# Ratio attention with double-buffered tiles, and its reciprocal as a logarithm, an exponential and a Newton step

## What is computed

```python
qkv = layernorm(x) @ w_qkv + b_qkv          # q, k, v
dot = q @ k.T                                # 32 x 32 for a head
den = |q|^2 + |k|^2 - 2*dot + 1e-6
score = dot*dot / den + causal_mask          # one division for each score
x = x + softmax(score) @ v @ w_out + b_out
```

## Time and profile before

| | before |
|---|---|
| median of 3 executions | 928.77 us (927.69 to 935.02) |
| the profiled execution, its own time | 933.23 us |
| its span, first to last instruction | 931.5 us |
| ratio attention in the span | 283.1 to 403.2 us |
| mean granted TensorE clock | 0.882 of full speed |
| TensorE, VectorE, ScalarE, GpSimd busy over the span | 75, 56, 39, 35% |

### The profile page before, as it was taken

The page is one execution under the profiler, slowest core; times in us unless marked ns, Lnnn a source line. Parts: engine busy times, 40 slices in busy tenths (PEclk is TensorE's granted clock), DMA queues, the critical chain, the costliest instruction groups (busy, mean ns, idle before and its releaser), DMA issues. The chain is left out here.

```text
span 931.5 us, 16522 instructions
## 1 busy us (share of the span) xinstructions
PE 701.1 (75%) x5634; PEld 523.2 (56%) x5634; DVE 523.1 (56%) x1424; ACT 358.7 (39%) x982; POOL 327.1 (35%) x442
## 2 busy tenths in 40 slices
PE   4889999999986666449900558997899964499994
PEld 3667777777765555344400446564677844266663
DVE  2666666767663799863496512333888844422221
ACT  1434545545542644223535503331566631022221
POOL 2145545454401544300527000001666411255542
PEclk9999999999995887668955687999999995599998
DMA  9823222222100000000000023776400002123331
GB/s 269 301 79 70 63 70 67 71 68 67 32 1 1 2 1 1 1 1 0 0 0 0 1 91 110 243 237 236 207 2 2 2 1 91 30 47 58 58 52 23
DMA packets 40091, 61.87 MB, mean 66 GB/s; under 512 B 6352, under 2 KB 28400, under 8 KB 39632
## 3 DMA queue, kind: packets, MB, share of 16 engines
q1 hardware_dynamic: 35600, 54.76, 19.3%
q0 software_dynamic: 4416, 6.13, 4.3%
HBM read 55.73 MB, written 5.14 MB: 65 GB/s over the span
## 5 line engine op out<-in xcount | busy, mean ns | idle before, releaser
L369 ACT ACTIVATE prob<-s_sb,negm 128x257 f32<-128x257 f32 x128 | 66.2, 517 | 99.3 <-DVE negm L560 99.3
L325 POOL TENSOR_SCALAR bias<-dist,cst 128x257 f32<-128x257 f32 x128 | 60.0, 489 | 112.5 <-DVE dist L547 98.8
L556 DVE CUSTOM_DVE_ANT_0 s_sb<-psum,bias 128x257 f32<-128x257 f32 x128 | 49.3, 423 | 72.6 <-PE psum L443 63.3
L2070 PE MATMUL psum<-ex_w,ex_rT 128*128 x184 | 62.8, 486 | 8.2 <-ACT ex_rT L1994 8.2
L1200 PE MATMUL psum<-ff_w_down_T,ff_gate 128*128 128x256 f32 x96 | 23.2, 408 | 57.7 <-DVE ff_gate L1271 57.7
L421 PE MATMUL psum<-ctxT,w_xa_k 128*128 128x257 f32 x256 | 62.3, 386 | 0.0
L429 PE MATMUL psum<-w_xa_v,ctxT 128*128 128x256 f32 x256 | 60.4, 379 | 0.0
L1959 POOL DMA_INDIRECT out<-ex_o,ex_target x23 | 36.4, 1583 | 57.2 <-ACT ex_o L2001 54.3
L1200 PEld LDWEIGHTS psum<-ff_w_down_T,ff_gate 128*128 128x128 f32 x96 | 19.8, 207 | 61.5 <-issue 58.5
L429 PEld LDWEIGHTS psum<-w_xa_v,ctxT 128*128 128x128 f32 x256 | 48.5, 189 | 6.8
L443 PE MATMUL psum<-kT,qbd 64*128 64x257 f32 x256 | 47.8, 433 | 4.3 <-DVE mx L556 4.3
(11 more groups left out here) (349 smaller groups left out, 1736.7 us busy)
## 6 DMA issues: line engine op xcount, KB each, us to landing
ctxT<-in_ctx_T SPq DMA_DIRECT2D x32, 257.0 KB
cx_ctxT<-in_ctx_T SPq DMA_DIRECT2D x32, 257.0 KB, 4.6
cx_ctx<-in_ctx SPq DMA_DIRECT2D x32, 256.0 KB, 4.0
ex_w<-in_w SPq DMA_DIRECT2D x1, 5632.0 KB, 17.1
kpos<-in_kpos SPq DMA_DIRECT2D x32, 128.5 KB
msk<-in_mask SPq DMA_DIRECT2D x32, 128.5 KB
ex_w<-in_w SPq DMA_DIRECT2D x1, 3072.0 KB, 24.1
x<-in_x SPq DMA_DIRECT2D x1, 1024.0 KB, 6.6
```

The source lines that it names most:

```text
L325: nc.gpsimd.tensor_scalar(bias[n % 2][:, g, :], dist[n % 2][:], c.slope[:, g:g + 1], 1.0, ALU.mult, ALU.mult).then_inc(bias_ready, 1)
L369: nc.scalar.activation(prob[n % 2][:, g, :], s_sb[n % 2][:, g, :], ACT.Exp, bias=negm[:, b, g:g + 1], accum_out=esum[t % 2][:, b, g:g + 1]) \
L556: nc.vector.tensor_tensor_reduce(s_sb[n % 2][:, g, :], sc[g % 2][:, 0:SK], bias[n % 2][:, g, :], 1.0, float("-inf"), ALU.add, ALU.max, mx[ ...
L2070: ins = nc.tensor.matmul(y_bank[part][:, 0:FE], rT[j % 2][:, k, :], ex.w1[:, bass.ds(e, 1), k, FE * part:FE * part + FE].rearrange("p a f ...
```

## The change

All tiles of the phase get two buffers (`xT` three), the slots start at -4 and are all written out, and the steps are put in another order in each stream. TensorE adds up the whole denominator in PSUM: four calls of `per_batch` for a tile in place of two and the |q|^2 products. ScalarE copies v out of PSUM without its bias; that bias goes once through `w_out` at the start (`wide`, `row`) and is added with `b_out`. ScalarE also copies the weighed values and their sums out of PSUM (`o_own`, `sums`), and VectorE multiplies from there. In place of VectorE's reciprocal of `den`, ScalarE makes `near` = exp(-ln(den)), and VectorE does one Newton step in two instructions. GpSimd spreads both halves of the keys. The core of the diff:

```diff
--- before.py
+++ after.py
@@ -816,238 +816,252 @@
...
+        xn, xT = [sb(f"xn{i}", [P, D]) for i in range(2)], [sb(f"xT{i}", [P, KT, P]) for i in range(3)]
...
+        FIRST = -4
...
             @block.gpsimd
...
+                for u in range(FIRST, NT + 1):
+                    if there(u + 4):
+                        pool.wait_ge(var_ready, u + 5)
+                        nc.gpsimd.tensor_tensor(rstd[u % 2][:], veps[u % 2][:], c.half[:, 0:1], ALU.pow) \
+                            .then_inc(rstd_ready, 1)
                     if there(u + 2):
...
+                        n = u + 2
+                        pool.wait_ge(k_ready, n + 1)
+                        at_least(pool, s_full, n - 1)
+                        for m in range(KT):
+                            ins = spread_heads(nc.gpsimd, kbd[n % 2][:, m, :, :, :], kT[:, m, :], c.head)
+                        ins.then_inc(kbd_ready, 1)
+                        pool.wait_ge(xn_ready, n + 1)
+                        pool.wait_ge(row_ready, 1)
+                        nc.gpsimd.tensor_tensor(x[:, n, :], x[:, n, :], row[:], ALU.add).then_inc(bias_added, 1)
                     if there(u + 1):
...
+                        n = u + 1
+                        pool.wait_ge(v_done, n + 1)
+                        at_least(pool, o_full, n - 1)
+                        spread_batches(nc.gpsimd, vbd[n % 2], v, c).then_inc(vbd_ready, 1)
+                        pool.wait_ge(square_ready, n + 1)
+                        pool.wait_ge(inverse_ready, n + 1)
+                        at_least(pool, p_ready, n - 1)
+                        nc.gpsimd.tensor_tensor(num[n % 2][:], square[n % 2][:], inverse[n % 2][:], ALU.mult) \
+                            .then_inc(ratio_ready, 1)
+                        pool.wait_ge(ratio_ready, n + 1)
+                        nc.gpsimd.tensor_tensor(num[n % 2][:], c.causal.unsqueeze(1).broadcast_to([P, NH, SQ]),
+                                                num[n % 2][:], ALU.subtract) \
+                            .then_inc(masked_ready, 1)
...
             @block.scalar
...
+                for u in range(FIRST, NT + 1):
+                    if there(u - 1):
+                        n = u - 1
+                        act.wait_ge(o_full, n + 1)
+                        at_least(act, o_ready, n)
+                        nc.scalar.copy(sums[:].rearrange("p (i b) -> p i b", b=BT), shares(o_banks)[:, :, :, 32])
+                        for h in range(4):
+                            mine, at = slice(SQ * h, SQ * h + SQ), DH * (h % 2)
+                            ins = nc.scalar.copy(o_own[mine, :].rearrange("p (b i d) -> p i b d", b=BT, i=NG),
+                                                 shares(o_banks)[mine, :, :, at:at + DH])
+                        ins.then_inc(o_read, 1)
+                    if there(u + 3):
+                        n = u + 3
+                        act.wait_ge(xT_full, n + 1)
+                        at_least(act, v_full, n - 2)
+                        nc.scalar.copy(xT[n % 3][:], x_bank[:, 0:D].rearrange("p (k t) -> p k t", k=KT)) \
+                            .then_inc(xT_done, 1)
+                    if there(u):
+                        act.wait_ge(sub_ready, u + 1)
+                        at_least(act, pT_ready, u - 1)
+                        nc.scalar.activation(prob[u % 2][:], num[u % 2][:], ACT.Exp).then_inc(p_ready, 1)
+                    if there(u + 2):
+                        n = u + 2
+                        act.wait_ge(qk_full, n + 1)
+                        at_least(act, kbd_ready, n)
+                        for m in range(KT):
+                            at = P * (KT + m)
+                            ins = nc.scalar.activation(kT[:, m, :], qk_bank[:, at:at + P], ACT.Identity,
+                                                       bias=w["ra_bqk"][:, KT + m:KT + m + 1])
+                        ins.then_inc(k_ready, 1)
+                        at_least(act, s_full, n - 1)
+                        for m in range(KT):
+                            at = P * m
+                            nc.scalar.activation(q2T[n % 2][:, m, :], qk_bank[:, at:at + P], ACT.Square,
+                                                 bias=w["ra_bqk"][:, m:m + 1])
+                            ins = nc.scalar.activation(qm2T[n % 2][:, m, :], qk_bank[:, at:at + P], ACT.Identity,
+                                                       bias=bq2[:, m:m + 1], scale=-2.0)
+                        ins.then_inc(qk_done, 1)
                     if there(u + 1):
                         n = u + 1
                         act.wait_ge(s_full, n + 1)
...
-                        nc.scalar.copy(in_banks(dot), s_banks[:, :, 0:D]).then_inc(s_read, 1)
+                        at_least(act, ratio_ready, n - 1)
+                        nc.scalar.activation(in_banks(square[n % 2]), s_banks[:, :, 0:D], ACT.Square, scale=0.5) \
+                            .then_inc(square_ready, 1)
+                        act.wait_ge(v_full, n + 1)
+                        at_least(act, vbd_ready, n)
+                        nc.scalar.copy(v[:], v_bank[:, 0:D]).then_inc(v_done, 1)
+                        act.wait_ge(s_read, n + 1)
+                        at_least(act, inverse_ready, n - 1)
+                        act_steps.link(act, nc.scalar.activation(near[n % 2][:], den[n % 2][:], ACT.Ln))
+                        nc.scalar.activation(near[n % 2][:], near[n % 2][:], ACT.Exp, scale=-1.0).then_inc(near_ready, 1)
                     if there(u + 2):
                         n = u + 2
...
+                        act.wait_ge(kbd_ready, n + 1)
+                        nc.scalar.activation(k2bd[n % 2][:], kbd[n % 2][:], ACT.Square).then_inc(k2_ready, 1)
...
             @block.tensor
...
-                            ins = nc.tensor.matmul(q_sums.rearrange("p (f m h) -> p f m h", f=2, m=KT)[:, :, m, :],
...
+                pe.wait_ge(consts_set, 1)
+                for k in range(KT):
+                    ins = nc.tensor.matmul(y_bank[:, 0:D], wide[:, k, :], w["ra_o"][:, k, :], start=(k == 0),
+                                           stop=(k == KT - 1))
+                ins.then_inc(row_full, 1)
+                ones = lambda lo, m, b: c.ones[lo:lo + 64, :]
+                heads = lambda lo, m, b: c.headq[lo:lo + 64, :]
+                for u in range(FIRST, NT + 1):
+                    if there(u + 3):
+                        n = u + 3
                         pe.wait_ge(xn_ready, n + 1)
...
+                        at_least(pe, xT_done, n)
+                        turn_tokens(nc, x_bank, xn[n % 2], c).then_inc(xT_full, 1)
                     if there(u + 2):
                         n = u + 2
                         pe.wait_ge(xT_done, n + 1)
                         at_least(pe, qk_done, n)
...
+                        project_qk(nc, qk_bank, w["ra_qkv"], xT[n % 3]).then_inc(qk_full, 1)
+                    if there(u - 1):
+                        n = u - 1
+                        pe.wait_ge(oT_ready, n + 1)
+                        pe.wait_ge(row_ready, 1)
+                        at_least(pe, y_done, n)
+                        project_tokens(nc, y_bank, oT[n % 2], w["ra_o"]).then_inc(y_full, 1)
+                    if there(u + 1):
+                        n = u + 1
+                        pe.wait_ge(kbd_ready, n + 1)
+                        pe.wait_ge(qk_done, n + 1)
+                        at_least(pe, s_read, n)
+                        at_least(pe, square_ready, n)
+                        per_batch(nc, s_banks, tokens(qm2T[n % 2]), heads_apart(kbd[n % 2]), 0, True)
+                        per_batch(nc, s_banks, tokens(qm2T[n % 2]), heads_apart(kbd[n % 2]), D, False)
+                        per_batch(nc, s_banks, tokens(q2T[n % 2]), heads, D, False)
+                        pe.wait_ge(k2_ready, n + 1)
+                        per_batch(nc, s_banks, ones, heads_apart(k2bd[n % 2]), D, False).then_inc(s_full, 1)
+                        at_least(pe, v_done, n)
+                        project_tokens(nc, v_bank, xT[n % 3], w["ra_qkv"][:, :, 2 * D:3 * D]).then_inc(v_full, 1)
                     if there(u):
                         pe.wait_ge(pT_ready, u + 1)
                         pe.wait_ge(vbd_ready, u + 1)
...
+                        at_least(pe, o_read, u)
+                        weigh_values(nc, o_banks, pT[u % 2], vbd[u % 2], c).then_inc(o_full, 1)
...
             @block.vector
...
+                def features(n):
+                    dve.wait_ge(o_read, n + 1)
+                    st.link(dve, nc.vector.reciprocal(rden[:], sums[:]))
+                    nc.vector.tensor_tensor(
+                        o[:].rearrange("p (b i d) -> p i b d", b=BT, i=NG),
+                        o_own[:].rearrange("p (b i d) -> p i b d", b=BT, i=NG),
+                        rden[:].rearrange("p (i b) -> p i b", b=BT).unsqueeze(3).broadcast_to([P, NG, BT, DH]),
+                        ALU.mult).then_inc(o_ready, 1)
```

(97 more changed lines are left out.)

157 lines of the change are left out of this document (16 added, 141 removed).

## The result

Over 20 executions of each, the kernel after takes 938.7 us and the kernel before 932.4 (medians): ratio 1.0063, 95% interval 1.0040 to 1.0086, so 3.7 to 8.0 us more. The profiled execution took 935.87 us, span 934.1.

The account below looks back on a forecast made before the run. VectorE set the pace before; afterwards a closed chain of waits through TensorE, partly at half clock, would. 23.5 + 12.6 + 88.2 (six at 14.7) + 14.0 = 138.3 us for 120.1; 18.2 added to 928.77 gives 947.0, range 932 to 958.

Parts of the forecast that it names:

- the chain through TensorE: Waits from one `near` to the next through output projection, score calls and v: 12.7 us at full clock, 14.7 forecast.
- four calls of 0.65: TensorE's four `per_batch` score calls per tile: 0.65 us each at full clock, 0.4 more each at half clock.
- the one through GpSimd: Waits from `near` through Newton step, GpSimd's product and mask, exponential and ScalarE's copies to the next `near`: 12.6 us.
- full clock throughout: Rival: TensorE's clock rises early and survives the pauses; six periods of 12.7, phase 5.2 us longer, 934 us; chance 0.17.
- The start: From the phase's start to the first landing of `near`: 23.5 us, between 22.5 and 24.5.
- The first period: Period between tiles 0 and 1, without an output projection: 12.6 us.
- the end from the last `near`: From the last tile's `near` to the end of the phase: 14.0 us, give or take 0.5.
- The loads: Two ScalarE table loads a tile, before logarithm and before exponential, both on the way to `near`, 1.283 us each.
- no loads in the slots: Rival: both functions found in one set, table switches cost nothing; 20.5 us go, 926.5 us; chance 0.03.
- the waits don't close: Rival: buffers decouple the streams, ScalarE's 9.4 us alone sets the period; phase 16.8 us shorter, 912 us; chance 0.08.
- the two rivals on the clock: TensorE at full clock throughout, 934 us, chance 0.17; or at half clock throughout, 957 us, chance 0.12.
- What lies outside the phase: Code surrounding the phase, taken as untouched, so the phase's 18.2 us was added to the median of 928.77 us.

Follow-up runs that it names:

- the pause filled: Kernel after, with 17 unused 128x128 products added in TensorE's pause ahead of each output projection; ratio to the kernel before 1.0020, phase 124.6 us.
- The kernel with three calls: Kernel after, without the `per_batch` call on `q2T`, so the denominator lacks the sum of q squared; 943.8 us in one execution, phase 128.2 us.
- the one in the old order: Kernel before, with only the reciprocal replaced by logarithm, exponential and Newton step, pipeline and order kept; ratio 1.0381, phase 159.1 us.

## Why the prediction came out as it did

The time of 938.7 lies in the range and on the side forecast, but the size is wrong: 18.2 us forecast, 5.9 measured (8.8 in the phase). That the time is only 8.3 us off the 947.0 is partly luck, since the forecast started from 928.8 (three executions) and the kernel before takes 932.4 over 20. The structure held, one price didn't. Of the 12.3 us by which the size is off, 9.4 lie in the phase (6.2 in the six periods, 2.9 in the start) and 2.9 outside it.

**The term that failed** is the four calls of `per_batch` in "the chain through TensorE", "four calls of 0.65" and 0.4 more for each at half clock, with two to three of them there. Every other piece of that chain came as costed: from `near` to the projection's start 3.67 (3.7), the projection at half clock to the first call 2.00 (1.05 + 0.95), v and its handoff 1.17 (1.15), v's copy, loads, logarithm and exponential 4.26 (4.2). The calls took 334.83 to 337.42 = 2.59, where 4 x 0.65 + 2.5 x 0.4 is 3.6. That is the whole miss of the period, 14.7 - 1.0 = 13.7. Two mistakes made it. The step of 0.65 at full clock came from a call that stands alone in front of v; inside a run a call follows after 0.44 (336.36 to 336.80), the last one ahead of v takes 0.62, and four in a row take 1.96 with the pause filled, not 2.6: 0.64 of the 1.0. The kernel with three calls bears this step out, 0.43 us for one call at the start. The rest is the half clock, which cost the calls 2.59 - 1.96 = 0.63, not 1.0. With calls at 1.96 the full-clock chain through TensorE is 12.1, below the one through GpSimd, so that full clock throughout is worth only 1.1 us a tile: that is what the filled pause gave.

**The start** was 20.6, not 23.5, for the same two causes: q and k of tile 1 ran at full clock (2.02, not 3.78), and the four calls from 295.58 to 297.54 took 1.96, not four times 1.0. The forecast stood between 24.5 at half clock and 22.5 with the clock risen (its own 305.1 less 283.1 is 22.0, a slip of 0.5); the clock rose earlier than either allowed for, before q and k of tile 1. The first period (12.48 for 12.6) and the end from the last `near` (13.7 for 14.0) held. In sum: 20.61 + 12.49 + 82.04 + 13.74 = 128.9.

**The loads** lay in the path at 1.283 each, as forecast; "no loads in the slots" didn't come by itself, but is what one line brings. **The rivals**: "the waits don't close" is refuted by a wait of 5.18 us for `ra_oT` in a slot. Of the two rivals on the clock neither came: it falls and returns in each slot, as forecast. That "full clock throughout", with 5.2 us, lies nearest to the 5.9 measured is luck.

**What lies outside the phase** I had put at no change. The program's median rose by 3.7 to 8.0 us, the phases by 8.8 and 9.3. By medians against phases (before 120.1), all eight timed kernels gained 1.1 to 5.7 us more, or lost so much less, over the program than in the phase, the one in the old order too (37.3 for 39.0). Single executions of the untouched code range from 803.5 to 813.8 us, more than this difference, so they name no cause; it stays open.

## What to carry to other kernels

Taking time off the fullest engine buys only what the next closed chain allows: write down that chain, through every engine's written order, before and after. An operation with two functions on ScalarE may carry a table load in front of each, here 2 x 1.28 us a tile on the critical chain; ask for a set that holds both. Price a short call in a run by the step from call to call in a run, not by its own length or from one that stands alone.

## What was not expected of the hardware

- A run of short calls (16 products of 64 x 32 x 128) steps at 0.44 us a call at full clock, while each call's row reads 0.69 to 0.70 and the last one ahead of v steps 0.62.
- Removing one of four such calls behind a pause left the period at 13.65 us, because the granted clock came back 4.2 us or more behind the projection's start and not 3.3.
- A table load cost its 1.283 us here and nothing beside: sixteen of them removed gave 20.2 us.
- A pass of VectorE over 128x512 took 1.31 us instead of 0.69, and one over 128x256 1.13 instead of 0.41, beside GpSimd's spreading of k, which itself took 2.49 instead of 2.04.
